# Attention beside an expert network: expert outputs issued in eight parts between score pairs, and VectorE's look for shares put in front of its wait for the turned rows

## The reference, cut to what matters

```python
xn = _layernorm(x)                                   # 4 x 2048 x 256
# attention, 16 heads of 16 columns
attn = softmax(einsum('bhqd,bhkd->bhqk', query, key) / scale)
out  = einsum('bhqk,bhkd->bhqd', attn, value)
# experts: each of 32 experts takes 8 tokens of a batch
probs = softmax(einsum('bsd,ed->bse', xn, gate_w) + gate_b, axis=-2)
vals, idx = top_k(probs over the tokens, 8)
merged = einsum('bked,bke->bed', xn[idx], vals)      # one row per batch and expert
h = gelu(einsum('bei,eih->beh', [merged, 1], w1))    # 1024 hidden columns
o = einsum('bej,ejo->beo', [h, 1], w2)               # 256 columns
out = zeros.at[idx].add(einsum('beo,bke->bkeo', o, vals))
x = x + s * silu(g)
```

## Time and profile before

| | us |
|---|---|
| median of 3 runs | 2803.9 |
| lowest and highest | 2802.91, 2807.53 |
| the profiled execution's own time | 2805.47 |
| its span, first to last instruction | 2803.7 |
| attention stage in the trace | 272 to 810 |
| PE busy in the span | 2542.8 (91%) |
| DVE busy | 2322.1 (83%) |
| ACT busy | 2013.0 (72%) |
| POOL busy | 2060.7 (74%) |

### The profile page before, as it was taken

One profiled execution on the slowest core, in us unless ns is written; L12 is line 12 of the kernel. 1 busy time (PEld: TensorE's weight loads), 2 busy tenths in 40 slices (PEclk: granted clock), 3 DMA queues, 4 the chain that ended last, 5 costly groups with the idle time before them and its releaser, 6 DMA issues.

```text
span 2803.7 us, 37402 instructions
## 1 busy us (share of the span) xinstructions
PE 2542.8 (91%) x13454; PEld 1489.0 (53%) x13454; DVE 2322.1 (83%) x2883; ACT 2013.0 (72%) x3253; POOL 2060.7 (74%) x682
## 2 busy tenths in 40 slices
PE   7897899999976899999999999999999999999978
PEld 3454344443443565656656566565655646556455
DVE  7685777777634999898998989989899898998995
ACT  4222466666634788787888978889788897888864
POOL 0656011111211999999999999999999999999996
PEclk9898899999978899999999999999999999999989
DMA  6347988888641131321313213132131321313210
GB/s 187 116 117 188 247 226 229 201 202 219 218 154 72 79 129 47 113 106 38 129 47 113 106 38 129 47 113 106 38 129 47 113 105 40 129 42 110 98 46 8
DMA packets 129505, 323.86 MB, mean 116 GB/s; under 512 B 15757, under 2 KB 84365, under 8 KB 112798
## 3 DMA queue, kind: packets, MB, share of 16 engines
q1 hardware_dynamic: 107050, 249.05, 28.9%
q0 software_dynamic: 19968, 71.38, 8.0%
q10 hardware_dynamic: 2304, 1.05, 0.2%
HBM read 286.75 MB, written 43.13 MB: 118 GB/s over the span
## 4 chain that ended last, share of the span: by engine, by line
POOL 32%; PE 20%; issue 13%; DVE 3%; ACT 1%; DMA 0%; POOLq 0%; DVEq 0%; SPq 0%; ACTq 0%
POOL l_st L1710 15%; POOL l_st L1702 9%; PE l_p_w L2163 6%; PE l_p_w L2104 5%; PE l_p_y L2088 5%; POOL keep_xg L1710 4%; POOL l_dtu L1716 2%; PE l_p_w L2182 2%; DVE l_st L1515 1%; POOL l_gate L1726 1%; DVE keep_xg L1515 1%; DVE keep_xg L1524 1%; PE l_p_w L2170 1%; PE l_p_w L2111 0%; ACT l_p_a L1798 0%
## 5 line engine op out<-in xcount | busy, mean ns | idle before, releaser
L1515 DVE TENSOR_TENSOR_SCAN l_st<-l_p_a,l_hl,l_st 128x512 f32<-128x512 f32 x768 | 932.3, 1265 | 105.7 <-ACT l_p_a L1798 95.5
L1710 POOL TENSOR_TENSOR l_st<-l_st,lw_cs 128x2048 f32<-128x2048 f32 x192 | 869.1, 4544 | 0.0
L1798 ACT ACTIVATE l_p_a<-l_dt,lw_a_neg 128x512 f32<-128x512 f32 x1024 | 664.9, 680 | 45.6 <-DVE keep_xg L1515 37.9
L1702 POOL TENSOR_TENSOR l_st<-l_bs,l_dtu 128x2048 f32<-128x2048 f32 x128 | 581.4, 4542 | 28.8 <-PE l_p_y L2088 25.4
L2088 PEld LDWEIGHTS l_p_y<-keep_ident,l_st 128*128 128x128 f32 x3072 | 354.4, 145 | 145.7 <-POOL l_st L1710 79.3
L2088 PE MATMUL l_p_y<-keep_ident,l_st 128*128 128x128 f32 x3072 | 384.4, 281 | 48.6 <-POOL l_st L1710 48.3
L1020 ACT ACTIVATE a_pr<-a_p_s 128x512 f32<-128x512 f32 x512 | 284.8, 596 | 145.8 <-PE a_p_s L1089 142.0
L931 DVE TENSOR_REDUCE a_mpart<-a_p_m 128x1 f32<-128x512 f32 x512 | 312.2, 681 | 14.1 <-PE a_p_m L1045 13.0
L1515 DVE TENSOR_TENSOR_SCAN keep_xg<-l_p_a,l_hl,keep_xg 128x512 f32<-128x512 f32 x256 | 314.7, 1266 | 1.6
L1710 POOL TENSOR_TENSOR keep_xg<-keep_xg,lw_cs 128x2048 f32<-128x2048 f32 x64 | 291.1, 4549 | 2.0 <-ACT l_hl L1803 2.0
L858 POOL DMA_DIRECT2D a_w<-in_w_dram x32 | 23.1, 725 | 328.8 <-PE a_p_m L1119 273.4
(11 more groups left out here) (246 smaller groups left out, 4027.3 us busy)
## 6 DMA issues: line engine op xcount, KB each, us to landing
l_bs<-s_bc SPq DMA_DIRECT2D x64, 1024.0 KB, 4.7
lw_cs<-s_bc SPq DMA_DIRECT2D x64, 1024.0 KB, 4.7
a_w<-in_w_dram POOLq DMA_DIRECT2D x32, 1024.0 KB, 11.7
late<-in_w_dram POOLq DMA_DIRECT2D x32, 1024.0 KB, 18.9
kx<-s_kp SPq DMA_DIRECT2D x96, 256.0 KB, 11.3
keep_share<-s_x SPq DMA_DIRECT2D x32, 512.0 KB, 5.1
s_kp<-late SPq DMA_DIRECT2D x96, 128.0 KB, 2.1
s_vp<-late SPq DMA_DIRECT2D x16, 544.0 KB, 3.5
```

What stands on the lines that cost most here:

```text
L1515: eng.tensor_tensor_scan(st[k % NG][:, n, :], p_a[:, n, :], st[k % NG][:, n, :], hl[:, k, n:n + 1], ALU.mult, ALU.add).then_inc(scan_ok, 1)
L1702: eng.tensor_tensor(st[n][:, :, :], bs[:, 4 * n:4 * n + 4, :], dtu[(k // NG) % 2][:, :].unsqueeze(1).broadcast_to([P, NG, TT]), ALU.mult). ...
L1710: eng.tensor_tensor(st[n][:, :, :], st[n][:, :, :], cs[:, 4 * n:4 * n + 4, :], ALU.mult).then_inc(cm_ok, 1)
L1798: eng.activation(p_a[:, n, :], dt[c % 2][:, :], ACT.Exp, scale=a_neg[:, c, m:m + 1]).then_inc(dA_ok, 1)
```

## The change

Three edits, all in the attention stage. `outputs` takes a range of blocks c, and in the odd passes 3 to 13 its eight blocks of four matmuls go behind the slots n = 5 to 12, one each, in place of all 32 behind slot 5. The copy of the result (`experts_out`) moves from in front of tile 8's maximum to in front of tile 18's. And VectorE's share computation is written ahead of its wait for the turned rows; this changes the order in the odd steps only (5 to 15), since an even step has no such wait.

```diff
-                        if i == 8 and hg % 2 == 0 and g > 2:
+                        if i == 18 and hg % 2 == 0 and g > 2:
                             experts_out(g // 2 - 2)
...
                     maxima(g, b, hg)
+                    if g == HG:
+                        eng.wait_ge(consts, 16 * 4)
+                    if g >= HG:
+                        one_choice(g - HG, b - 1, hg)
                     if hg % 2:
                         eng.wait_ge(hTp_ok, q + 1)
...
-                    if g == HG:
-                        eng.wait_ge(consts, 16 * 4)
-                    if g >= HG:
-                        one_choice(g - HG, b - 1, hg)
                     take(*prev(g, b, hg))
...
-                            if c == 1 and hh == 1 and hg % 2 and 1 < g < G - 1:
-                                outputs(b * QB + hg // 2 - 1)
+                            if 5 <= n < 13 and hg % 2 and 1 < g < G - 1:
+                                outputs(b * QB + hg // 2 - 1, (n - 5,))
...
-                def outputs(q):
-                    wait(eng, eo_ok, q)
-                    eng.wait_ge(w2_in, q * 64 + 64)
-                    eng.wait_ge(hg_ok, q + 1)
-                    for c in range(8):
+                def outputs(q, blocks):
+                    for c in blocks:
+                        if c == 0:
+                            wait(eng, eo_ok, q)
+                            eng.wait_ge(w2_in, q * 64 + 64)
+                            eng.wait_ge(hg_ok, q + 1)
                         for j in range(4):
                             i = eng.matmul(p_e[32 * j:32 * j + B, 0:D], hT[q % 2][:, c, j, :], w2[:, j, c, :], start=c == 0, stop=c == 7)
-                    i.then_inc(o_ok, 1)
+                        if c == 7:
+                            i.then_inc(o_ok, 1)
```

More of the change, by code:

```diff
@@ L1105, in weigh @@
                         if c == 4 and g == G - 2:
-                            outputs(QUADS - 2)
+                            outputs(QUADS - 2, range(8))
                         if c == 5 and g == G - 1:
-                            outputs(QUADS - 1)
+                            outputs(QUADS - 1, range(8))
                     values(7)
```

## The result

The changed kernel takes 2810.45 us (median of 16 runs, 2806.15 to 2815.14), the kernel before 2803.89 us in 16 runs of its own: a ratio of 1.0025, 95% interval 1.0017 to 1.0032. It is slower by a quarter of a per cent. The prediction said 2813.6, from 2805.0 to 2817.0.

The account below looks back on a forecast made before the run. TensorE's order was taken to set the pace. Six odd-pass stretches go from 376.75 to 386.40 us (five at 64.67, one at 63.05), +9.7 on 2803.9, giving 2813.6 us, range 2805.0 to 2817.0.

Parts of the forecast that it names:

- The shares fit into the wait: VectorE, odd steps: shares take 3.3 us and fit the 9.1 us wait for turned rows, over 5 us spare.
- The parts leave the hole: Odd passes: only the first part stands in ScalarE's pause between slots 5 and 6; seven come behind slots 6 to 12.
- The price of seven parts: TensorE behind slots 6 to 12: seven parts cost 4.16 us, less 0.40 hidden, leaving 3.76 us on the path.
- the two ways to price a switch of form: TensorE's seven parts: 4.16 us with a drain at each mode change, 3.01 us without.
- What is hidden: TensorE, slots 8 to 16: parts fill some 0.4 us of waits for ScalarE, 0.2 in each group of four.
- The falls: Half clock behind a 2.04 us gap before slot 6, in five of six odd passes, 1.62 us each.
- The loads: GpSimd's next w2 load starts 5 to 7 us later; no price, as the DMA engines have idle time.
- the clock did fall: Rival: the 2.04 us gap before slot 6 does not bring the clock down; +1.6 us, 2805.5; chance 0.14.
- the parts were not cheap: Rival: TensorE's parts cost 0.43 us each, seven 2.61 after hiding; +2.8 us, 2806.7; chance 0.08.
- the faster case: Rival: seven parts cost 2.41 us, clock stays up, a third wait is filled; -6.6 us, 2797.3; chance 0.06.
- the dearer case: Rival: clock falls in all six odd passes and no wait is filled; +13.7 us, 2817.6; chance 0.10.
- The shares' own gain: Passes 5 to 13 become like pass 3: 1.67 us gap in slot 5 removed, output block back between slots 5 and 6.

Follow-up runs that it names:

- the one-piece kernel: Changed kernel with all eight output parts put back behind slot 5, shares' move and late copy kept; 2786.59 us, ratio 0.9938 to the kernel before.
- the filled pass 1: Kernel before with shares moved, outputs in one piece, plus 22 unread wide matmuls behind slot 5 of pass 1; 2783.82 us, ratio 0.9924.
- the shares' move alone: Kernel before with only VectorE's share computation put ahead of its wait for the turned rows; 2783.86 us, ratio 0.9927.
- four parts: Changed kernel with outputs in four parts of eight matmuls behind slots 5 to 8; 2799.72 us, ratio 0.9989 to the kernel before.
- at the values: Changed kernel with four parts of eight matmuls directly in front of the values in slots 7, 11, 15, 19; 2811.28 us, ratio 1.0024.
- six and two: Changed kernel with six output blocks behind slot 5, one each before the values in slots 11 and 15; 2787.63 us, ratio 0.9942.
- the fill: Changed kernel with 18 unread wide matmuls behind the first part, in slot 5 of odd passes 3 to 13; 2802.88 us, ratio 0.9999.
- the parts alone: Changed kernel with the share computation put back behind the bias addition, outputs still in eight parts; 2812.53 us, ratio 1.0038 to the kernel before.

## Why the prediction was right, and where it was off

- **The shares fit into the wait.** Shown: 9.12 us became 5.80, and alone the edit gives 16.4 us in the stage, the 16.2 that follow from passes 5 to 13 going like pass 3.
- **The parts leave the hole.** Shown: the one-piece kernel has all else of the change and is 23.6 us faster in the stage. The edit for VectorE had put the block back into the hole; the edit for TensorE took it out.
- **The price of seven parts.** 3.76 us was the forecast. By the slots it is 12.39 - 8.72 = 3.67; by the stretches 62.96 - 59.33 = 3.63, with the filled pass 1 as the measure of two passes without outputs (59.29 in the prediction). The terms hold singly: 0.55 us for a part (0.56), 0.09 in front (0.10), and about 0.4 hidden. Of the two ways to price a switch of form, the fixed price for each piece won: without it the stretch would have been 61.9. The Trainium skill's rule that a change of tiling mode drains TensorE (TensorEngine Tiling (Array Packing), Key Properties) agrees with this; the rows show a fixed time at each switch (0.09 us in front, 0.55 - 0.43 = 0.12 behind), not what TensorE does in it.
- **What is hidden** was right in size: 0.4 us, one wait of 0.2 us in each of the groups of slots 8 to 11 and 12 to 15. But not each part fills a wait; its place decides. The kernel with the shares' move alone has in slots 13 and 14 of pass 5

```profile
464.35 0.38 PE L1089 MATMUL a_p_s<-q,kx 99*128 99x256 bf16 x2
464.57 0.38 PE L1045 MATMUL a_p_m<-kx,a_qst 96*128 96x512 bf16 x1
464.98 0.39 PE L1089 MATMUL a_p_s<-q,kx 99*128 99x256 bf16 x2
```

with 0.41 us from the score tile to slot 14, which waits for the exponential of slot 12. In the changed kernel (pass 3) a single part stands behind slot 12, between the two:

```profile
407.20 0.61 PE L1137 MATMUL a_p_e<-late,a_hT 128*4 128x256 f32 x8
407.74 0.39 PE L1089 MATMUL a_p_s<-a_qst,kx 99*128 99x256 bf16 x2
407.97 0.38 PE L1045 MATMUL a_p_m<-kx,q 96*128 96x512 bf16 x1
408.19 0.38 PE L1089 MATMUL a_p_s<-a_qst,kx 99*128 99x256 bf16 x2
```

Here it is 0.22 us: this part filled the wait. The parts of the other kernels that filled none stand ahead of the pair whose exponential is awaited (four parts), or behind the wait of their group (at the values, six and two).

- **The falls.** Five of six was the forecast, four came in the profiled execution (none in passes 3 and 13); each cost about 1.6 us, as forecast. This count is the term that was most off: with four falls of 1.58 and parts at 3.65 us the sum is 6 x (59.29 + 3.65) + 4 x 1.58 - 376.75 = +7.2, as the trace shows. All six passes have the same gap of 2.16 us in front of slot 6, so the forecast could not have named the four, and that the count came out near it is partly luck. That the gap is the cause was argued before and is shown by the fill.
- **The loads.** GpSimd issued the w2 load of pass 5 at 472.69, 19.0 us behind the bias addition (12.0 before), and no wait of TensorE for it appeared: from 380 to 760 us its list of waits holds only waits for ScalarE.

The rivals fell as follows: the clock did fall, the parts were not cheap, the faster case needed cheap parts and a clock that stays up, and the dearer case needed six falls and nothing hidden. The shares' own gain, up to 16 us, was seen in the prediction as making passes 5 to 13 like pass 3, but never priced alone; it is what the change could have had.

## What to carry to other kernels

When two edits touch one wait, price each by itself and against the other: here one was worth 16 us and the other threw it away with 7 more. A long block that looks clumsy may be what fills a hole of another engine (here two table loads on ScalarE); before cutting it up, look at what else would stand there. And small pieces of another matmul form had a fixed price here, 0.2 us each beside their work. A piece fills a wait of a two-buffer exchange only if it stands between the step whose result is awaited and the step that waits.

## What the runs showed of the hardware

The clock fell behind gaps that were not long, and not each time. Over all kernels, behind gaps in front of slot 6: 2.7 us, all nine first passes without a fill and five of six in the kernel with the parts at the values; 2.16 us, four of six in the changed kernel; 1.73 us, two of six. Where the gap was filled or covered by the block, no pass fell. Gaps of 1.67 us in slot 5 (the kernel before and the kernel with the parts alone): three of five and four of five. Which of equal gaps was followed by a fall could not be foreseen.

A fall can last longer. In the kernel with the parts alone, pass 9 (same columns as all stretches):

```profile
586.00:588.00 2.00, 2.00 (x12) 0.45 (x12) 2.00 (x5) 1.39 (x3) 0.00 (x0) 0.50 0.99 184
588.00:590.00 2.00, 2.00 (x13) 0.44 (x12) 1.23 (x2) 0.60 (x1) 0.00 (x0) 0.50 1.03 162
590.00:592.00 2.00, 2.00 (x19) 0.62 (x20) 0.69 (x1) 0.60 (x1) 0.00 (x0) 0.50 1.04 201
592.00:594.00 2.00, 2.00 (x28) 0.58 (x19) 0.51 (x1) 0.60 (x1) 0.00 (x0) 0.92 1.02 195
```

The clock stays at 0.50 for over 6 us although TensorE is busy throughout, and this stretch is 2.75 us longer than the one at full clock, not 1.6. Passes 5 and 13 of this kernel and pass 3 of the one with the parts at the values have such a dear fall too (a mean clock of 0.95 over the stretch). Why it stayed low was not tried.
